# Last stage of a graph kernel: one VectorE instruction for the shift of a pair of tiles, and GpSimd adding in one tile of four

## The reference, cut to what matters

```python
# u: attention messages summed per node and projected (0 for a node with no edge)
out = x1 + u                                   # node_feat + out
mean = out.mean(axis=0)
var = jnp.mean(jnp.square(out - mean), axis=0)
out = (out - mean) * rsqrt(var + EPS) * gamma + beta      # per column
x   = x1 + out
x   = (x - mean_of_row(x)) / sqrt(var_of_row(x) + 1e-5)    # _layernorm
```

## Time and profile before

| | |
|---|---|
| median of 3 runs | 1443.65 us (1442.55 to 1444.2) |
| the profiled execution's own time | 1441.92 us |
| its span in the trace | 1440.2 us |
| the last stage's loops in it | from about 1292.5 us to the end |
| TensorE busy over the span | 1340.0 us (93%) |
| VectorE, ScalarE, GpSimd busy | 1093.7, 593.2, 826.0 us |
| mean granted TensorE clock | 0.97 of full speed |
| DMA engines' busy share from 1300 us, in stretches of 20 us | 1.05, 0.99, 0.94, 0.72, 0.55, 0.56 |

### The profile page before, as it was taken

One profiled execution on the slowest core, in us unless ns is written; L12 is line 12 of the kernel. 1 busy time (PEld: TensorE's weight loads), 2 busy tenths in 40 slices (PEclk: granted clock), 3 DMA queues, 4 the chain that ended last, 5 costly groups with the idle time before them and its releaser, 6 DMA issues. The chain is left out here.

```text
span 1440.2 us, 22074 instructions
## 1 busy us (share of the span) xinstructions
PE 1340.0 (93%) x6660; PEld 1075.8 (75%) x6660; DVE 1093.7 (76%) x2043; ACT 593.2 (41%) x1107; POOL 826.0 (57%) x766
## 2 busy tenths in 40 slices
PE   6888978999999949999999999999999999859997
PEld 5677766887888738888888888888888888744443
DVE  5467646888888722588888888888888888968897
ACT  2367542555555521222222222222222222246786
POOL 3355515666666534356666666666666665468785
PEclk9999998999999979999999999999999999869999
DMA  8777746666666442344444444444444443849955
GB/s 285 277 234 247 246 176 203 223 214 225 219 218 219 165 135 87 103 133 132 133 133 132 132 132 132 132 132 132 132 132 132 132 132 88 285 137 366 318 196 186
DMA packets 128302, 257.97 MB, mean 179 GB/s; under 512 B 21459, under 2 KB 21907, under 8 KB 128114
## 3 DMA queue, kind: packets, MB, share of 16 engines
q1 hardware_dynamic: 97778, 175.83, 36.8%
q0 software_dynamic: 29920, 80.38, 17.9%
q10 hardware_dynamic: 544, 1.05, 0.2%
HBM read 197.18 MB, written 73.60 MB: 188 GB/s over the span
## 5 line engine op out<-in xcount | busy, mean ns | idle before, releaser
L205 PE MATMUL pse<-w_lo,w_hi 128*128 128x512 f32 (+2 forms) x1140 | 416.6, 365 | 21.2 <-DVE w_lo L1407 17.6
L206 PE MATMUL pse<-w_hi,w_lo 128*128 128x512 f32 (+2 forms) x1140 | 411.4, 361 | 0.0
L207 PE MATMUL pse<-w_hi 128*128 128x512 f32 (+2 forms) x1140 | 411.1, 361 | 0.0
L205 PEld LDWEIGHTS pse<-w_lo,w_hi 128*128 128x128 f32 x1140 | 217.9, 191 | 53.8 <-DVE w_lo L1407 18.0
L207 PEld LDWEIGHTS pse<-w_hi 128*128 128x128 f32 x1140 | 217.5, 191 | 32.3
L206 PEld LDWEIGHTS pse<-w_hi,w_lo 128*128 128x128 f32 x1140 | 217.8, 191 | 30.0
L1153 POOL TENSOR_TENSOR acc_x<-acc_x,node_rows 128x512 f32<-128x512 f32 x72 | 116.6, 1619 | 77.7 <-DMA node_rows<-x_table 73.5
L842 POOL TENSOR_TENSOR node_y<-node_z,node_x 128x512 f32<-128x512 f32 x79 | 101.9, 1290 | 100.7 <-issue 79.4
L205 PE MATMUL psn<-w_lo,agg_hi 128*128 128x512 f32 x316 | 125.4, 397 | 0.0
L207 PE MATMUL psn<-w_hi,agg_hi 128*128 128x512 f32 x316 | 125.4, 397 | 0.0
L206 PE MATMUL psn<-w_hi,agg_lo 128*128 128x512 f32 x316 | 125.3, 397 | 0.0
(11 more groups left out here) (259 smaller groups left out, 2924.5 us busy)
## 6 DMA issues: line engine op xcount, KB each, us to landing
node_x<-in_x SPq DMA_DIRECT2D x79, 256.0 KB
x_table<-node_x SPq DMA_DIRECT2D x79, 256.0 KB, 2.0
node_rows<-x_table SPq DMA_DIRECT2D x79, 256.0 KB, 8.2
coef_all<-coef_table SPq DMA_DIRECT2D x38, 512.0 KB
ea_rows<-in_ea SPq DMA_DIRECT2D x40, 256.0 KB
edge_part<-part SPq DMA_DIRECT2D x40, 256.0 KB
sum_table<-sums SPq DMA_DIRECT2D x40, 256.0 KB
out_dram<-rows_over_w_lo SPq DMA_DIRECT2D x40, 256.0 KB
```

What stands on the lines that cost most here:

```text
L205: pe.matmul(to, left[0], right[1], start=first, stop=False)
L206: pe.matmul(to, left[1], right[0], start=False, stop=False)
L207: return pe.matmul(to, left[0], right[0], start=False, stop=last)
```

## The change

Two edits, both in `finish_stage`. `by_pool` names tiles with `j % 4 == 1` instead of `j % 8` in 1, 4, 6: 20 GpSimd tiles in place of 30, and so 59 plain tiles in place of 49. And the shift of a pair of tiles is one `scalar_tensor_tensor` over both, `(mean * -1.0) * rstd`, in place of one `tensor_scalar` for each tile. It reads `mv` and `rstd` as two tensors, where `tensor_scalar` read `mv` as a tensor and `rstd` as a scalar per partition. The semaphore counts on `scale_ok` follow: two per pair instead of three, and ScalarE waits for the pair's shift, not for each tile's.

```diff
         def by_pool(j):
-            return j % 8 in (1, 4, 6)
+            return j % 4 == 1
...
                     if j >= 0:
-                        act.wait_ge(scale_ok, 3 * (j // 2) + 2 + j % 2)
+                        act.wait_ge(scale_ok, 2 * (j // 2) + 2)
...
                     if pair:
-                        dve.wait_ge(scale_ok, done // 2 + done // 2 * 2 + 1)
-                        for i in range(m, m + n):
-                            v.tensor_scalar(bias[:, i, :], mv[:, i, 0:1], rstd[:, i, :], -1.0, ALU.mult, ALU.mult).then_inc(scale_ok, 1)
+                        dve.wait_ge(scale_ok, done // 2 * 2 + 1)
+                        v.scalar_tensor_tensor(bias[:, m:m + n, :], mv[:, m:m + n, 0:1], -1.0, rstd[:, m:m + n, :], ALU.mult, ALU.mult).then_inc(scale_ok, 1)
```

## The result

| | before | changed kernel |
|---|---|---|
| median, the same chip, 7 runs each | 1441.92 us (1441.17 to 1444.2) | 1448.08 us (1443.31 to 1448.8) |
| ratio of the changed kernel to before | | 1.0034, 95% interval 1.0021 to 1.0046 |
| span of the profiled execution | 1440.2 us | 1446.8 us |
| TensorE, start of tile 2 to start of tile 78 | 134.12 us | 141.12 us |

Slower, by 0.2 to 0.5%. The loss lies in the loops of the last stage: TensorE needs 7.0 us more from tile 2 to tile 78, 4.6 of them before tile 47 and 2.4 behind it. Two smaller terms lead from there to the 6.6 us of span: tile 2 starts 1.2 us earlier, which nothing in the change explains, and tile 78 is now plain, 0.86 us longer.

A forecast was written before the change was run, and what follows sets the result against it. GpSimd was taken as the bound, 13.96 us per eight tiles of the last stage. Fewer adds +1.1 us and the merged shift 0 gave 1443.0 us, on the median 1444.8 us; range 1442.0 to 1448.5 us.

The forecast's parts named there:

- The likeliest case: Whole kernel: +1.1 us, so 1444.8 us, likely span 1443.5 to 1446 us; chance 0.60.
- the first rival: Last stage: the new shift waits on VectorE for GpSimd's add; +4.1 us, 1447.8 us; chance 0.19.
- What bounds the kernel: Last stage, eight tiles: GpSimd sets the pace at 13.96 us; TensorE needs 13.02, VectorE 12.24 us.
- Edit 1: Fewer GpSimd adds in the last stage: the bound moves to TensorE at 13.88 us for eight tiles; +1.1 us.
- The stops by late gathers: Last stage, before about 1360 us: three waits of TensorE, carried over from the old trace, cost 2.5 us.
- the walk: TensorE followed from tile 2 at its new pace, with three stops: end at 1434.4 us against 1433.32.
- Edit 2, what it saves: One VectorE shift instruction less per pair, hidden in the aggregation's wait for statistics: 0.01 us each, taken as 0.
- Edit 2, what it adds: The merged shift on VectorE in the last stage, taken as costing 0; meeting an add left to chance, 18%.
- rival 1: Last stage: new shift held by GpSimd's add, 0.97 us or a whole add, +0.6 to +6.5 us; chance 0.19.
- the scans: Four VectorE scans took 6.55 us beside GpSimd's adds, 2.68 us with GpSimd idle: 0.97 us each.
- Rivals 2 to 4: Last stage: TensorE free, -1.4 us, 0.13; VectorE was the bound, -4.7 us, 0.03; GpSimd stays bound, +3.0 us, 0.05.

## Why the prediction was right or wrong

The range held the time (1448.08 us, at its upper end). The likeliest case did not happen; the first rival did, which had 0.19. That the time lies in the range is luck in part: the prediction put 1.7 us on everything, since the median of three runs (1443.65 us) lay that much above the profiled execution. The median of seven is 1441.92 us, that execution's own time. Without the 1.7 us the range would have ended at 1446.8 us, below the measured time.

- **What bounds the kernel**: right. GpSimd was the bound at 13.96 us, TensorE stood at 13.02. With the adds alone changed, TensorE's round is 6.93 us against the 6.94 worked out.
- **Edit 1**: right in its mechanism, somewhat high in its size. The sum said +1.1 us with bounds of -1.4 and +1.1; measured, the ratio 0.9995 is -0.7 us, with 1.4 us either way, so inside the bounds, with the +1.1 chosen from them just outside. The stops by late gathers were somewhat less than I carried over: tile 2 to tile 78 took 133.65 us, where the walk gives 134.4.
- **Edit 2, what it saves**: right, nothing. The old pair lay in the wait for the statistics: with one free shift the aggregation starts 0.81 us after them (1386.78 to 1387.59), with two it was 0.83.
- **Edit 2, what it adds**: wrong, and this is the step that failed. "Removing one gives 0.01 us ... 0" took the new instruction as harmless, and left the hold to chance: "by chance 18% of the shifts meet one, for half its length". Measured: every second shift from the second pair on to near the end, most of them for the whole add and a little more. Here the two engines met by phase, not by chance: 18 of 35 shifts in this kernel, 0 of 40 with the adds one tile later.
- **The price in rival 1**: its lower end, 0.97 us from the scans, was too small a wait; the hold is 1.54 - 0.14 = 1.40 us. Its upper end, "with a whole add of 1.28 us, 7.28 us", is near VectorE's 7.33, but the sum isn't right as it stands. It takes off 0.12 us for one instruction, where four tiles have two pairs and lose two, and by the prediction's own reading of the earlier trace rows neither counts; by the rows it is 6.07 us and a loss of 1.25. The 0.34 us x 19 = 6.5 us of that end is near the 7.0 us that TensorE lost, in part by chance too, since 4.6 of them were lost before tile 47, where holds and late gathers mix. The whole rival, +4.1 us with three us for the hold, lies inside what was measured: +4.9 us by the ratio (3.0 to 6.6), +6.2 by the medians.
- **The Trainium skill's rules**: "SBUF — State Buffer", Who interferes with whom: a VectorE instruction with two SBUF inputs is shut out while GpSimd reads SBUF. The trace agrees in each part that was tried: two tensors from SBUF are held, a tensor and a scalar per partition are not, one tensor from SBUF and one from PSUM are not (L1431), and without an add nothing is. "VectorE: DVE Perf Modes", Rules for kernel authors, to minimise the count of instructions: here the merged instruction, one less for each pair, cost 0.3 to 0.5%, for what it reads and not for the count.
- **Rivals 2 to 4**: TensorE didn't run free of the late gathers with the adds alone changed (133.65 us from start of tile 2 to start of tile 78, where no wait at all would give 57 x 1.95 + 19 x 1.09 = 131.9), nor did VectorE pay back an instruction; GpSimd was in time, as worked out.

## What to carry to other kernels

Before an operand that was a scalar per partition becomes a tensor, look what GpSimd does beside that instruction: with two SBUF tensors a 0.14 us instruction here took 0.4 to 1.7 us when it met an add, and once 1.97. When two engines run in one loop of semaphores, work out the phase between them rather than a chance of meeting; and as the phase can move with what is moved, try it: adds one tile later took the whole loss away, while the shift 0.6 us earlier still met the add, which came along, and lost its place in a wait besides. Balance by the engines' times for a round: 1.30 and 2.45 us on GpSimd, 1.95 and 1.09 us on TensorE put the best share of adds near one in three (the two engines' times are equal at 0.32). Two kernels with 26 of 79 were faster, by 0.2 to 0.3%, where the tiles are 2 and 4 of six; with every third tile the gain isn't clear of noise.

## What the runs showed of the hardware that I had not expected

- The shift is held by an add that, by the trace, starts after it: shift at 1383.10, add at 1383.33, and a free shift takes 0.14 us. The widest case is in the run of the shift alone:

```profile
1361.70 1.97 DVE L1946 SCALAR_TENSOR_TENSOR fin_bias<-fin_mv,fin_rstd 128x2 f32<-128x2 f32 x1
```

```profile
1361.35 1.00 POOL L1813 DMA_INDIRECT rows_over_w_lo<-msg_table,last_edge  x1 [0.30 <-DVE rows_over_w_lo L1933]
1362.37 1.27 POOL L1819 TENSOR_TENSOR rows_over_w_lo<-rows_over_w_lo,fin_x_more 128x512 f32<-128x512 f32 x1
```

  The shift starts 0.67 us ahead of the add's recorded start, while GpSimd still issues the gather in front of it, and ends with the add (1363.67 and 1363.64). It is no exception. In five profiles with the new operand (the changed kernel twice, the shift alone, the shift earlier, two shifts of two tensors) 64 shifts (where they come in pairs, pairs) start inside the issue of a gather, or at its end, with an add right behind it, within 0.03 us: all 64 are held to the add's end, whatever the time between. Over all nine profiles with the new operand 135 start inside the issue of a gather with another gather next: none is held. Whether GpSimd takes the way to SBUF for the add while the gather is still being issued, or the add's start is recorded late, no run here tells.
- A hold ends within about 0.04 us of the add's end in all the rows shown of single shifts, whatever the shift's start: 1.97, 1.54, 1.34, 1.03 and 0.59 us by where it met the add.
- Two tensors aren't the only form that is held. The copy of one tensor in the earlier trace rows, 128x4 from SBUF to SBUF, took 1.09 us beside GpSimd's adds and 0.17 us with GpSimd idle:

```profile
L1364 DVE COPY carry<-v_turned x19: 170/1093/1103, 616.0 to 1254.9; 128x4 f32<-128x4 f32 x19
```
